# Joining two blocks of a three-stage kernel: the mLSTM cell and the shared experts in one instruction block, with the first token chunk of the experts placed ahead of the cell's last batch pairs

## What is computed

```python
x = x + tanh(g_xattn[0]) * mlstm_cell(layernorm(x), ctx, ctx)     # 8 heads of 32
x = x + tanh(g_ffn[0])   * ffn0(layernorm(x))                     # 2 shared experts + 8 routed, top 2
x = x + tanh(g_xattn[1]) * attention(layernorm(x), ctx)           # 16 heads of 16
x = x + tanh(g_ffn[1])   * ffn1(layernorm(x))

# inside the cell, per sequence and head
D_mat = exp(log_D - max_log_D);  C = q @ k.T / sqrt(32) * D_mat
normalizer = max(abs(C.sum(-1)), exp(-max_log_D))
h = (C / (normalizer + EPS)) @ v
out = (h - mean(h)) / sqrt(var(h) + LN_EPS) * ln_scale            # over the 256 features
# inside ffn0, for every token
shared = sum(silu(x @ w1.T) * (x @ w3.T) @ w2.T for the two shared experts)
logits = x @ router.T + bias;  the two largest, softmax over them, weight the two chosen experts
```

## Time and profile before

| what | value |
|---|---|
| median of 3 runs | 842.37 us (839.71 to 842.46) |
| profiled execution, its own time | 842.14 us |
| span of the profiled execution | 840.3 us |
| busy share PE, DVE, ACT, POOL | 93%, 58%, 47%, 27% |
| mean granted TensorE clock | 0.982 |
| cell, first score matmul to last `turn_back` | 36.35 to 87.9 us |
| first shared gate matmul | 103.27 us |
| first indirect DMA of the scatter | 180.06 us |
| first gate matmul of the routed tiles | 252.40 us |

### The profile page before, as it was taken

How to read it: one execution, slowest core, us unless ns; L and a number is a source line. 1 busy time by engine, 2 the same in 40 slices (tenths; PEclk the granted TensorE clock), 3 DMA queues, 4 the chain that set the end, 5 groups by cost and what they waited for, 6 DMA issues and landing times.

```text
span 840.3 us, 15738 instructions
## 1 busy us (share of the span) xinstructions
PE 780.4 (93%) x5412; PEld 628.7 (75%) x5412; DVE 485.9 (58%) x1607; ACT 398.7 (47%) x817; POOL 228.2 (27%) x208
## 2 busy tenths in 40 slices
PE   8668899999999999999999889998889999999997
PEld 7456487788887888888887545655668878888886
DVE  5488865465474333343333676767676666756544
ACT  5598455144462222222223488888835344243222
POOL 0069210037601222232224248765300000000000
PEclk9989999999999999999999999999999999999999
DMA  8478640024252333433332700202004022050140
GB/s 303 143 267 305 259 192 1 1 94 146 86 186 70 66 66 64 85 74 66 63 51 27 233 1 15 89 2 76 2 4 100 1 67 61 1 127 2 33 94 26
DMA packets 37516, 74.51 MB, mean 89 GB/s; under 512 B 4448, under 2 KB 25568, under 8 KB 35680
## 3 DMA queue, kind: packets, MB, share of 16 engines
q1 hardware_dynamic: 30288, 64.16, 24.5%
q0 software_dynamic: 7152, 9.34, 6.3%
HBM read 59.76 MB, written 19.01 MB: 94 GB/s over the span
## 4 chain that ended last, share of the span: by engine, by line
PE 42%; DVE 14%; issue 13%; ACT 7%; POOL 5%; DMA 4%; DVEq 3%; POOLq 1%; SPq 0%; ACTq 0%
PE t_y_ps L2292 8%; POOL slot_tokens L1694 4%; PE a_turned L999 3%; PE a_score L977 2%; PE t_up L2273 2%; PE t_up L2274 2%; PE t_up L2272 2%; PE a_score L979 2%; PE a_score L978 2%; ACT a_hhi L1175 2%; PE t_gate L2262 2%; PE t_gate L2263 2%; PE t_gate L2264 2%; PE a_turned L903 2%; PE a_proj L876 2%
## 5 line engine op out<-in xcount | busy, mean ns | idle before, releaser
L2232 POOL DMA_INDIRECT sums<-t_y,t_dest x39 | 60.9, 1561 | 167.3 <-DMA sums<-t_y,t_dest 95.7
L2327 ACT CAST t_xT_hi<-t_x_turned 128x256 fp32r<-128x256 f32 x39 | 14.5, 372 | 139.0 <-PE t_x_turned L2253 139.0
L2292 PE MATMUL t_y_ps<-W,t_hidT 128*128 x312 | 73.8, 379 | 0.8 <-ACT t_hidT L2337 0.8
L1175 ACT CAST a_hhi<-a_hid 128x512 fp32r<-128x512 f32 x48 | 29.7, 620 | 86.8 <-DVEq L1461 85.2
L2292 PEld LDWEIGHTS t_y_ps<-W,t_hidT 128*128 128x128 f32 x312 | 59.0, 189 | 10.5 <-issue 1.0
L1307 DVE CUSTOM_DVE_ANT_0 a_sc<-a_score,a_pen 128x128 f32<-128x128 f32 x256 | 56.4, 285 | 7.9 <-PE a_score L891 6.7
L1463 DVE TENSOR_TENSOR a_hlo<-a_hid,a_hhi 128x512 fp32r<-128x512 f32 x48 | 33.3, 693 | 35.1 <-ACT a_hhi L1175 35.1
L1164 ACT ACTIVATE a_act_g<-a_score 128x512 f32<-128x512 f32 x48 | 28.7, 597 | 46.7 <-PE a_score L979 46.5
L2356 DVE TENSOR_TENSOR t_hid<-t_act_g,t_up 128x512 f32<-128x512 f32 x39 | 28.0, 718 | 36.6 <-ACT t_act_g L2332 32.8
L832 POOL TENSOR_TENSOR a_sc<-a_nmx,a_sc 128x512 f32<-128x512 f32 x32 | 33.4, 1043 | 45.2 <-DVE a_nmx L1307 45.1
L2348 DVE TENSOR_TENSOR t_xT_lo<-t_x_turned,t_xT_hi 128x256 fp32r<-128x256 f32 x39 | 16.6, 425 | 43.1 <-ACT t_xT_hi L2327 43.1
(11 more groups left out here) (428 smaller groups left out, 2261.6 us busy)
## 6 DMA issues: line engine op xcount, KB each, us to landing
W<-in_w_dram SPq DMA_DIRECT2D x9, 1536.0 KB, 8.0
a_cb<-comb_rows SPq DMA_DIRECT2D x16, 512.0 KB, 8.5
W<-m_rows SPq DMA_DIRECT2D x14, 512.0 KB, 4.9
slot_tokens<-in_blank_rows_dram SPq DMA_DIRECT2D x1, 5031.0 KB, 19.8
t_x<-slot_tokens SPq DMA_DIRECT2D x39, 129.0 KB, 2.6
a_raw<-in_w_dram SPq DMA_DIRECT2D x3, 1536.0 KB, 7.5
X<-in_x_dram SPq DMA_DIRECT2D x4, 512.0 KB, 6.1
ctxT_all<-in_ctxT_dram SPq DMA_DIRECT2D x4, 512.0 KB, 8.9
```

The source lines that it names most:

```text
L1175: act.copy(hhi[u % 2][:], hid[u % 2]).then_inc(hhi_ready, 1)
L2232: pool.indirect_dma_start(sum_dram, bass.IndirectOffsetOnAxis(ap=dest[p][:, 0:1].bitcast(U32), axis=0), y[p][:], None, compute_op=ALU.add) ...
L2292: last = pe.matmul(y_ps[p][:, 0:D], hidT[p][:, h], W[:, ds(e, 1), at:at + D], start=(h == 0), stop=(h == HT - 1))
```

## The change

Cell and shared experts are put into one block; `cell` hands three of its helpers and seven of its semaphores to `shared_feed_forward`. `finish` becomes `take` (denominator and scaling; pairs 0 to 4 stay in PSUM, pairs 5 to 7 are written to h in SBUF, which frees the PSUM at once) and `measure` (statistics and the subtract-and-scale). On VectorE the order is now: `weights(7)`; 1/std of pairs 0 to 4; addition, statistics and normalising of chunk 0; `take(5)`; `keep_lo` of chunk 0; `measure(5)`; `take(6)`, `take(7)`; step 0; `measure(6)`, `measure(7)`. ScalarE takes the cell's square roots in three parts. Chunk 1 goes the way of chunks 2 and 3 (ScalarE scales, GpSimd adds). Chunk 1's halves come at u = 6 instead of 3, the router at u = 10 instead of 8, the choice at 11 to 15; `positions` and `slot_weights` now both stand at u = 14.

GpSimd splits three weight pieces before its first exponents and five after its last; the raw weights' DMA is issued in `front`, behind `val`. TensorE's filler matmuls (6 after the cell, 5 and 2 before chunk 0) become 2. The first `gate_up` starts on the high halves alone. The third store goes ahead of SP's wait for the scatter. GpSimd's three drains behind `homes` become waits on a semaphore that its own copies raise. PSUM tiles of the three parts are laid so that they follow one another, and the banks of the y sums change.

```diff
@@ cell @@
-            for i in range(BY_DVE, PAIRS):
-                exponents(i)
-                if i == min(SPLIT):
-                    pool.wait_ge(raw_loaded, 16)
-                done = sum(SPLIT.get(past, 0) for past in range(i))
-                for n in range(done, done + SPLIT.get(i, 0)):
-                    piece(n)
+            pool.wait_ge(raw_loaded, 16)
+            for n in range(EARLY):
+                piece(n)
+            for i in range(BY_DVE, PAIRS):
+                exponents(i)
+            for n in range(EARLY, PIECES):
+                piece(n)
...
-            for _ in range(6):
-                pe.matmul(pvT[0][:], cst[:, C_ID:C_ID + 128], cst[:, 0:512], start=True, stop=True)
...
+            deviation(act, 0, IN_PSUM)
             for i in (PAIRS - 2, PAIRS - 1):
                 keep_out(i)
-            for first, end in ((0, PAIRS - 1), (PAIRS - 1, PAIRS)):
-                act.wait_ge(var_ready, end)
...
-                if i >= 2:
-                    finish(i - 2)
-            for i in (PAIRS - 2, PAIRS - 1):
-                finish(i)
+                if 2 <= i < PAIRS - 1:
+                    take(dve, i - 2)
+                    measure(dve, i - 2)
@@ shared_feed_forward @@
+            sp.wait_ge(cmat_ready, PAIRS)
             for e in range(under_tokens, 5):
+                if e == 4:
+                    sp.wait_ge(pv_ready, 2 * PAIRS)
...
-            store(0)
-            store(1)
+            for c in range(3):
+                store(c)
             for p in range(2):
                 sp.wait_ge(scattered[p], 16 * B // 2)
                 sp.wait_ge(scattered2[p], 16 * B // 2)
-            store(2)
...
-            pool.drain()
+            pool.wait_ge(rows_ready, 2)
...
-                pool.drain()
+                pool.wait_ge(rows_ready, 3 + part)
...
+                if u == 0:
+                    pe.wait_ge(split_done, 1)
+                    pe.wait_ge(hi_ready, 2)
...
+                if u < 2:
+                    pe.wait_ge(back_free, PAIRS - 2 + u)
...
-            busy(5)
+            busy(2)
             turn(0, 0)
             turn(0, 1)
-            busy(2)
             gate_up(0)
...
-            dve.reciprocal(hrstd[:], hstd[:])
-            dve.drain().then_inc(hrstd_ready, 1)
+            cell_rstd(1, 0, PAIRS - 3)
             add_h(0)
             statistics(0)
             normalise(0)
-            add_h(1)
+            take(dve, PAIRS - 3)
             keep_lo(0, 0)
             keep_lo(0, 1)
-            statistics(1)
+            measure(dve, PAIRS - 3)
+            take(dve, PAIRS - 2)
+            take(dve, PAIRS - 1)
             for u in range(NU):
...
                 if u == 0:
-                    statistics(2)
+                    cell_rstd(2, PAIRS - 3, PAIRS - 2)
+                    measure(dve, PAIRS - 2)
+                    measure(dve, PAIRS - 1)
```

More of the change, by code:

```diff
@@ L1625, in shared_feed_forward @@
         expert_f, expert_c = (raw1[0:1, 1536 + 64 * n:1536 + 64 * n + NT] for n in range(2))
-        gate, up = two(pb, "gate"), two(pb, "up")
+        gate, up = zip(*[(pb(f"gate{q}"), pb(f"up{q}")) for q in range(2)])
         y_bank = [pb(f"y{n}") for n in range(3)]
@@ L1764, in gate_up @@
                 xhi, xlo = (x_halves[:, c, half] for half in range(2))
+                if u == 0:
+                    for dst, cols in ((gate, gate_cols), (up, up_cols)):
+                        for k in range(KT):
+                            pe.matmul(dst[q][:], whi[:, cols(k, ht)], xhi[:, k], start=(k == 0), stop=False)
+                            pe.matmul(dst[q][:], wlo[:, cols(k, ht)], xhi[:, k], start=False, stop=False)
+                    pe.wait_ge(lo_ready, 2)
+                    for dst, cols in ((gate, gate_cols), (up, up_cols)):
+                        for k in range(KT):
+                            last = pe.matmul(dst[q][:], whi[:, cols(k, ht)], xlo[:, k], start=False, stop=(k == KT - 1))
+                    last.then_inc(gu_ready, 1)
+                    return
                 for dst, cols in ((gate, gate_cols), (up, up_cols)):
@@ L1876, in _ @@
             keep_hi(0, 1)
-            block1_hi(1)
-            deviation(1, 2)
+            unscale(1)
+            cell_deviation(act, PAIRS - 3, PAIRS - 2)
             for u in range(NU):
@@ L2064, in split_lo, with cell_rstd @@
                                   ).then_inc(wlo_ready, 1)
-            dve.reciprocal(hrstd[:], hstd[:])
-            dve.drain().then_inc(hrstd_ready, 1)
+            def cell_rstd(nth, first, end):
+                dve.wait_ge(hstd_ready, nth)
+                dve.reciprocal(hrstd[:, 2 * first:2 * end], hstd[:, 2 * first:2 * end])
+                dve.drain().then_inc(hrstd_ready, 1)
+            cell_rstd(1, 0, PAIRS - 3)
             add_h(0)
@@ L2188, in routed_tiles @@
         hid = two(sb, "hid", [128, HID])
-        gate, up, y_ps = two(pb, "gate"), two(pb, "up"), two(pb, "y_ps")
-        x_turned, h_turned = pb("x_turned"), pb("h_turned")
+        gate, up = zip(*[(pb(f"gate{p}"), pb(f"up{p}")) for p in range(2)])
+        y_ps0, x_turned, y_ps1, h_turned = pb("y_ps0"), pb("x_turned"), pb("y_ps1"), pb("h_turned")
+        y_ps = [y_ps0, y_ps1]
         x_loaded = two(sem, "x_loaded")
```

233 lines of the change are left out of this document (131 added, 102 removed).

## The result

| | before | after |
|---|---|---|
| median | 842.38 us (839.34 to 844.51, 20 runs) | 838.12 us (836.32 to 843.49, 20 runs) |
| profiled execution, its own time | 842.14 us | 838.09 us |
| span; mean granted clock | 840.3 us; 0.982 | 836.3 us; 0.980 |

The ratio after to before is 0.9959, with a 95% interval of 0.9947 to 0.9971. The changed kernel is faster by 0.41%, 3.5 us (2.4 to 4.5). That is clear of zero, but just inside the 0.5% that the prediction took as its bound. The forecast was 836.8 us, with a range of 832.8 to 841.2; it gave 0.63 to a gain of more than 0.5% and 0.31 to a smaller one, which is what came.

A forecast was written before the change was run, and what follows sets the result against it. The start of the routed tiles, where TensorE is busy 209.2 of 210 us, was taken to move the end; VectorE held the 16.6 us before the shared experts. 842.14 - 4.2 - 1.1 = 836.8 us, range 832.8 to 841.2.

The forecast's parts named there:

- Step 1: Start of the shared experts: chunk 0 goes ahead of the last pairs, so the first `gate_up` starts 11.6 us earlier.
- Step 2: Chunk 0, steps 0 to 9: TensorE waits 11.5 us, 4.1 of earlier waits fall inside; 4.2 us ahead at the router.
- The steady steps hand that on: Shared experts from the router's start on: the steady steps pass on TensorE's head start of 4.2 us.
- Step 3: Three weight pieces ahead of GpSimd's first exponents in the cell: zero effect, with 0.3 us either way.
- Step 4: Scatter: starts 1.3 us later, three drains gone save 3.1, ends 1.8 earlier; W[0] issued at about 230.4, soon enough.
- Step 5: Third store ahead of the scatter's wait: ScalarE's 1.62 us wait goes, the run to the token tile moves up 1.1 us.
- B: Chunk 0: the waits overlap, so half of TensorE's added waits vanish; 833.1 us, chance 0.14.
- C: Scatter ends too late: the drains' removal brings nothing, W[0] and W[1] land 3.1 us later; 838.5 us, chance 0.18.
- D: ScalarE's two extra table switches cost up to 2.8 us more than walked; 839.6 us, chance 0.03.
- E: TensorE's clock falls at chunk 0: 853.5 us if held four steps, a short dip costs 2 us; chance 0.05.
- F: Chunk 0 starts early, but the cell's leftovers or `gate_up(0)` waiting for GpSimd give all back; 842.1 us, chance 0.10.

The follow-up runs named there:

- the jump undone: Changed kernel with pairs 5, 6 and 7 finished ahead of chunk 0 again and fillers on TensorE: 846.73 us, 1.0067 of the kernel before.
- the tail parts on the kernel before: Kernel before with only the third store ahead of the scatter's waits and semaphores for GpSimd's three drains: 841.21 us, 0.9987.
- without the tail parts: Changed kernel with GpSimd's three drains back and the third store behind the scatter's wait: 843.32 us, 1.0016 of the kernel before.
- its twin: Changed kernel with one idle SP instruction more, the wait ahead of the load of W[7] standing twice: 839.99 us, 0.9960.
- Three kernels: Changed kernel with, one each: W[7] loaded behind two stores, 1.0162; four fillers in step 2, 1.0112; two pieces of VectorE's work moved later, 1.0146.

## Why the prediction held, point by point

**Step 1** held: the gate starts 11.7 us earlier, forecast 11.6, and VectorE's ends were within 0.5 us of the walk. In three of ten executions the gate is 1.5 later, by the wait for ScalarE's square root behind `keep_out` of pair 7 that this step ruled out. Two small errors met: the last `weights` ended 0.3 later, and `measure(5)` took 2.7 instead of 2.1, since its last operation takes 1.63 beside GpSimd's `add` where 0.88 is usual.

**Step 2** held in its sum: 7.2 us lost between gate and logits, forecast 7.4. Its parts did not. TensorE's waits were 8.0 us where the clock did not dip, and not 11.5; before had 3.1 and not 4.1. So 4.9 were added, and not 7.4. Single ones came out at 2.0 (forecast 1.6), 1.9 (2.5), 0.7 (1.0) and 1.0 (1.8). Another 2.2 us lie in matmuls that read longer, which the walk had not counted: 58.97 busy against 56.74. The list was also added up wrong. Its items make 11.5 and not 11.0; with the 0.5 for handovers that is 12.0, a head start of 3.7 and a forecast of 837.3. And with the jump undone 4.0 of the 7.2 remain, which the step had set against the jump. That the sum came within 0.2 us is in good part luck: too many waits, too few long matmuls and the slip cancel.

**"The steady steps hand that on"** is the sentence that failed. The head start fell from 4.5 to 2.8 us, 1.6 of it through two waits that the walk, ended at step 9, never reached: 0.72 at `down(15)`, with `positions` and the slot weights of u = 14 ahead of it on VectorE, and 0.83 at 199.15 for the store of chunk 1. The second is in no row of the kernel before, but its cause is: the store travels behind W[7] (the slowest store took 10.7 us there too), and ScalarE now comes for it earlier. The runs with W[7] later took the wait away: their stores landed in 5 us or less, and SiLU 20 came 106.6 to 106.9 us after the first gate instead of 107.2 to 108.0.

**Step 3** held. The early pieces cost 0.27 at the end of the cell, against the 0.3 allowed. One row was off: GpSimd's exponents of pair 3 started at 47.52 instead of 46.03, since two of the three pieces' roundings took 2.87 us beside VectorE's `exponents`; the one between, beside `weights`, took 0.83:

```profile
37.64 2.87 POOL L411 TENSOR_TENSOR sw0hi<-W,cst 128x384 fp32r<-128x384 f32 x1
41.60 0.83 POOL L411 TENSOR_TENSOR sw0hi<-W,cst 128x384 fp32r<-128x384 f32 x1
47.52 4.54 POOL L424 TENSOR_TENSOR W<-W,cst 128x2048 f32<-128x2048 f32 x1
```

**Step 4.** The slot weights were ready at 179.8, forecast 179.7. The drains were undersized, by a misread row: the 2.77 of the earlier trace rows are idle time behind the copies, and not from one DMA to the next, so taking the copies off again was wrong. The three places give 2.49 (2.77 to 0.28), 2.22 (2.50 to 0.28) and 0.64 (0.94 to 0.30), 5.3 us in all where 3.1 was taken. The scatter takes 43.5 us from first to last DMA instead of 49.4; 1.1 of these 5.8 lie in the DMAs' and copies' own durations. W[0] was issued at 228.0, forecast 230.4.

```profile
203.51 0.98 POOL L1711 DMA_INDIRECT slot_tokens<-W,slots  x1 [0.28 <-POOL W L1708]
```

**Step 5** mis-sized its term. ScalarE's SiLU came 1.07 us earlier by it, as said. But TensorE was not 1.1 late before: it had run ahead and its only wait there was 0.8 us, now 0.5. The SiLUs behind it followed at 4.0 and 3.4 us and so caught up. At the tile turn the term gave 0.35, not 1.1; the tail parts on the kernel before gave 0.4 there.

**The sum**: 4.5 - 1.6 + 0.35 is 3.2 us, and 3.15 is what the tile turn shows; the median ratio gives 3.5. The forecast of 5.3 was 2.1 above the tile turn: 1.3 by the head (4.5 where 4.2 was forecast, less the 1.6 of the waits not reached) and 0.75 by step 5. It also took 5.3 us for 0.66%; that is 0.63% of 842.14.

**The rivals.** B was half right in its mechanism, fewer waits of TensorE, and wrong in its time. C is refuted: the drains brought 5.3 us of their bound of 6.3. By the run with the drains back, W[0] issued at 234.2 would have been early enough as well. D is refuted: a SiLU follows its table load at once, at 94.91 behind a load of 1.28 that began at 93.62. By this, the rule of the Trainium skill, "ScalarE: Activation LUTs", section "What ACT_TABLE_LOAD costs", of a further 1.38 us is not seen here either. E happened in small: the clock dipped behind the gap, for under 4 us, and cost nothing, since TensorE waited the less; a dip ahead of chunk 0, which E did not look at, cost 1.5. F had a true core: without the tail parts the joined block gains nothing.

## What to carry to other kernels

A head start won early in a stage is worth what the later fixed events leave of it. Walk the schedule through to the stage's last handover, and look for transfers whose start does not move with the work: a consumer that comes earlier meets them as new waits. Two edits that cure the same wait are not to be summed: here they were worth 0.4 to 1.1 us together on one kernel and 4.8 on the other, where either one alone was as good as both. Where a stretch is bound by two vector engines that hand over to TensorE, as this one seems to be, neither dips of TensorE's clock nor fillers changed its length. Run an edit beside the kernel that it edits, on the same chip, before its loss or gain is put down to it.

The version that came out best is the change with W[7] loaded behind two stores and the drains kept, 838.03 us at 0.9943; against the change's 0.9959 the intervals overlap, and only the profile's places (0.6 to 1.5 us at the first routed gate, counted from the first gate, against three executions of the changed kernel and its twin) say that it is better. That is little more than those executions differ among themselves.

## What the runs showed of the hardware that was not expected

- TensorE, ScalarE and VectorE can stand still for 15 to 20 us beside a run of indirect DMAs on GpSimd, with no wait that the profile names. Three kernels did so in their profiled execution, and all 6 executions of each were long (850.37 us or more). All three ran on one chip; whether the chip, the edits or the missing drains set it off is open. Whoever times an edit near such a scatter should look at this stretch before judging the edit.
- GpSimd's and VectorE's two-input operations stretch each other where both read SBUF alone: a rounding of 384 columns took 2.87 for 0.83 us beside `exponents`, a pair of subtract-and-scale 1.63 for 0.88 beside `add`, and two low halves 3.42 beside `add`, where one alone takes 1.22. Beside `weights`, which reads one input from PSUM, the rounding kept its 0.83.
- A drain of GpSimd between a run of indirect DMAs and the next costs 2.2 to 2.5 us more than a wait on a semaphore that its copies raise (2.77 and 2.50 against 0.28). Ahead of the first DMA of all it costs 0.64 (0.94 against 0.30).
- A store of half a MB landed after 10 us when it was issued behind a load of 1.5 MB. Issued ahead of that load it took 2.9 to 4.6 us, with the scatter running beside it in both cases.
- The granted clock's dips fall in other places in other executions of the same head: at 96 to 104, 106 to 110 or 108 to 112 us, or nowhere between gate and logits, and in some at 82 to 84. The first four left the 67.0 us from gate to logits as they were; the last moved the gate by 1.5 us.
